# Routing weights that travel with the rows: ScalarE scales the expert results, the combining stages only add

## What is computed

```
x = LN(x + attn0(x))      # 16 heads, a band of 33 keys, a residual inside
x = LN(x + moe0(x))       # 16 experts, 4 chosen, softmax weights, GELU, hidden width 512, biases
x = LN(x + attn1(x))      # linear attention with decay, residual inside
x = LN(x + moe1(x))       # 8 experts, 2 chosen, softmax weights, SiLU gate times up, hidden width 512
# an expert layer:
#   w = softmax(top_k(logits));  result[row] = sum over k of w[row, k] * expert[topi[row, k]](x[row])
# moe1 also multiplies by 12 ** -0.5
```

## Time and profile before

| | |
|---|---|
| median of 3 runs | 1002.17 us (1000.47 to 1005.12) |
| profiled execution, its own time | 1005.16 us |
| its span, first to last instruction | 1003.3 us |
| PE busy | 737.3 us, 73% |
| DVE busy | 652.7 us, 65% |
| POOL busy | 548.0 us, 55% |
| ACT busy | 488.0 us, 49% |
| mean granted TensorE clock | 0.856 |

### The profile page before, as it was taken

One profiled execution on the slowest core, in us unless ns is written; L12 is line 12 of the kernel. 1 busy time (PEld: TensorE's weight loads), 2 busy tenths in 40 slices (PEclk: granted clock), 3 DMA queues, 4 the chain that ended last, 5 costly groups with the idle time before them and its releaser, 6 DMA issues.

```text
span 1003.3 us, 34835 instructions
## 1 busy us (share of the span) xinstructions
PE 737.3 (73%) x11638; PEld 601.2 (60%) x11639; DVE 652.7 (65%) x1988; ACT 488.0 (49%) x1174; POOL 548.0 (55%) x568
## 2 busy tenths in 40 slices
PE   2789889789987108999999991746664189999900
PEld 1466566566666107999899891634553179988900
DVE  4356667577756405777777775778775357777756
ACT  2355546456555105666666660223322257777713
POOL 1022176386568764677777772377767624445433
PEclk9799989899999558999999995776676589999965
DMA  7011121121222233343434433143332233222253
GB/s 219 2 45 35 29 73 53 39 82 50 65 68 76 69 111 81 77 87 80 89 84 87 90 66 127 51 131 100 108 104 73 86 63 67 63 53 55 51 162 99
DMA packets 135794, 78.97 MB, mean 79 GB/s; under 512 B 104338, under 2 KB 116793, under 8 KB 135696
## 3 DMA queue, kind: packets, MB, share of 16 engines
q1 hardware_dynamic: 121808, 50.97, 20.8%
q0 software_dynamic: 13312, 25.31, 8.0%
q10 hardware_dynamic: 576, 1.34, 0.4%
HBM read 32.34 MB, written 32.63 MB: 65 GB/s over the span
## 4 chain that ended last, share of the span: by engine, by line
PE 57%; DVE 13%; issue 12%; POOL 10%; ACT 3%; DMA 3%; SPq 1%; POOLq 0%; DVEq 0%; ACTq 0%
PE avbank L1676 7%; POOL xs L636 7%; PE proj L1676 7%; PE avbank L1527 4%; PE s L1655 3%; PE s L1656 3%; PE s L1657 3%; PE t L1656 3%; PE t L1655 3%; PE t L1657 3%; PE t L1721 3%; DVE nm L790 2%; PE t L1514 2%; PE proj L1433 2%; PE s L1477 2%
## 5 line engine op out<-in xcount | busy, mean ns | idle before, releaser
L702 POOL DMA_INDIRECT yt<-ysb,to_now x224 | 229.1, 1023 | 162.6 <-ACT ysb L1307 87.4
L636 POOL DMA_INDIRECT xs<-x1p,sidx x192 | 187.6, 977 | 55.2 <-issue 48.2
L930 DVE CAST h_hi<-act_out 128x512 bf16<-128x512 f32 x152 | 70.5, 464 | 77.3 <-ACT act_out L1320 74.2
L1655 PE MATMUL s<-xt,w_hi 128*128 128x256 bf16 x296 | 81.8, 276 | 42.5 <-DMA xt<-xs 42.5
L931 DVE TENSOR_TENSOR h_lo<-act_out,h_hi 128x512 bf16<-128x512 f32 x152 | 106.3, 699 | 5.2
L619 POOL TENSOR_TENSOR w_lo<-w_raw,w_hi 128x512 bf16<-128x512 f32 (+1 forms) x32 | 37.1, 1158 | 112.5 <-ACT w_hi L1291 112.2
L1221 ACT ACTIVATE prob<-t 128x384 f32<-128x384 f32 (+1 forms) x160 | 73.1, 510 | 35.8 <-PE t L1514 35.7
L1676 PE MATMUL avbank<-w_hi,h_hi 128*128 x448 | 81.1, 220 | 1.3 <-issue 0.8
L1657 PE MATMUL s<-xt,w_lo 128*128 128x256 bf16 x296 | 81.9, 277 | 0.0
L1656 PE MATMUL s<-xt,w_hi 128*128 128x256 bf16 x296 | 81.9, 277 | 0.0
L1655 PE MATMUL t<-xt,w_hi 128*128 128x256 bf16 x296 | 81.3, 275 | 0.0
(11 more groups left out here) (230 smaller groups left out, 2025.1 us busy)
## 6 DMA issues: line engine op xcount, KB each, us to landing
w_raw<-w_all SPq DMA_DIRECT2D x56, 256.0 KB
gat<-yt SPq DMA_DIRECT2D x8, 1024.0 KB, 5.8
gat<-yt SPq DMA_DIRECT2D x8, 512.0 KB, 4.2
yt<-ysb,to_now POOLq DMA_INDIRECT x224
xs<-tail_rows SPq DMA_DIRECT2D x24, 129.0 KB, 2.6
xs<-x1p,sidx POOLq DMA_INDIRECT x192, 2.8
out<-ow SPq DMA_DIRECT2D x8, 256.0 KB, 2.3
xt<-xs SPq DMA_TRANSPOSE x112
```

The lines of the kernel that those rows point to most:

```text
L636: pool.indirect_dma_start(out=xs[n][:, :], out_offset=bass.IndirectOffsetOnAxis(sidx[:, par, at:at + 1], 0), in_=x1p[:, par, t, k, :], in_ ...
L702: pool.indirect_dma_start(out=yt[n][:, :], out_offset=bass.IndirectOffsetOnAxis(to_now[:, u, s:s + 1], 0), in_=ysb[:, u, s, :], in_offset= ...
L930: ch.link(dve.tensor_copy(h_hi[:, par, c, :], act_out[:, par, c, :]))
L1655: pe.matmul(dst, w_h, xt[:, u, 0, :], start=True, stop=False)
```

## The change

Each row copy carries two 32-bit words, its number and its weight; `weigh` writes the weight into `x1p` beside the number. `load_numbers` brings both words into `to_now`. ACT's `take_out` waits for that load and scales as it takes the results out of PSUM: two instructions of 128x128 with a scale for each partition, in place of one copy of 128x256. The results in `yt` are weighted already, so that `combine` becomes three wide additions (`pair_up`: 128x1024, `add_up`: two of 128x512) and `final_sums` two additions of 128x512. `wres` and `wsel` are gone. `weigh` ends with one more `link`.

```
-XW = 2 * D + 2
+XW = 2 * D + 4
+NO = slice(2 * D, 2 * D + 2)
+WT = slice(2 * D + 2, XW)
...
-        to_now = sb("to_now", [P, RING, S2], U32)
+        to_now = sb("to_now", [P, RING, S2, 2], U32)
...
-        xs = [nc.dram_tensor(f"xs{n}", [experts[n] * REGION, XW], BF16).ap() for n in range(2)]
+        xs = [nc.dram_tensor(f"xs{n}", [experts[n] * REGION, XW // 2], U32).ap() for n in range(2)]
...
-                        sp.dma_start(to_now[:, u, :],
-                                     xs[n][bass.ds(row, TILE), 2 * D:XW].bitcast(U32).rearrange(
-                                         "(s p) o -> p (s o)", s=S2)).then_inc(to_loaded[n][u], 16)
+                        sp.dma_start(to_now[:, u, :, :],
+                                     xs[n][bass.ds(row, TILE), D:XW // 2].rearrange(
+                                         "(s p) o -> p s o", s=S2)).then_inc(to_loaded[n][u], 16)
...
+            pool.memset(tail_rows[:, :, WT], 0.0)
...
-                dve.tensor_tensor(wres[:, bass.ds(b * T, T), 0:k_n], etop[:, :, 0:k_n], bc(rsum[:, :], 2, k_n), ALU.mult)
+                ch.link(dve.tensor_tensor(x1p[:, par, :, 0:k_n, WT].bitcast(F32), etop[:, :, 0:k_n].unsqueeze(3),
+                                          bc(rsum[:, :], 2, k_n).unsqueeze(3), ALU.mult))
...
+            def add(dst, a, other):
+                return dve.scalar_tensor_tensor(out=dst, in0=a, scalar=1.0, in1=other, op0=ALU.mult, op1=ALU.add)
+
+            def pair_up(count, par):
+
+                dve.wait_ge(gathered[0][par], 16 * count)
+                ch.link(add(gat0[:, par, :, 0:2, :], gat0[:, par, :, 0:2, :], gat0[:, par, :, 2:4, :]))
+
+            def add_up(b, par):
+                ch.link(add(y[:, :, :], gat0[:, par, :, 0, :], xres[:, bass.ds(b * T, T), :]))
+                add(y[:, :, :], gat0[:, par, :, 1, :], y[:, :, :]).then_inc(comb_done, 1)
+                dve.wait_ge(comb_done, b + 1)
...
-                    combine(0, b + 2, i + 2, par, (0, 1))
+                    pair_up(i + 2, par)
...
-                    combine(0, b + 2, i + 2, par, (2, 3))
+                    add_up(b + 2, par)
...
-                for k in range(K1):
-                    for t in range(T):
-                        before = xres[:, b * T + t, :] if k == 0 else yf[:, par, t, :]
-                        ins = dve.scalar_tensor_tensor(out=yf[:, par, t, :], in0=gat1[:, b % FIN, t, k, :],
-                                                       scalar=wres[:, b * T + t, k:k + 1], in1=before,
-                                                       op0=ALU.mult, op1=ALU.add)
-                    if k < K1 - 1:
-                        ch.link(ins)
+                ch.link(add(yf[:, par, :, :], gat1[:, b % FIN, :, 0, :], xres[:, b * T:(b + 1) * T, :]))
+                ins = add(yf[:, par, :, :], gat1[:, b % FIN, :, 1, :], yf[:, par, :, :])
...
-                    nc.scalar.copy(ysb[:, u, :, :], y_bank[u % 2][:, 0:S2 * D].rearrange("p (s d) -> p s d", s=S2)
-                                   ).then_inc(y_done[n], 1)
+                    act.wait_ge(to_loaded[n][u], 16 * use + 16)
+                    for s in range(S2):
+                        ins = nc.scalar.activation(ysb[:, u, s, :], y_bank[u % 2][:, s * D:(s + 1) * D], ACT.Identity,
+                                                   scale=to_now[:, u, s, 1:2].bitcast(F32))
+                    ins.then_inc(y_done[n], 1)
```

More of the change, by code:

```diff
@@ L61 @@
 DEPTH_SCALE = 12.0 ** -0.5
-DVE_STEPS = 21
+DVE_STEPS = 22
 STACK_BANK = [1, 0] * 4
-DVE_STEPS_1 = 20
+DVE_STEPS_1 = 19
 C_IDENT, C_NEG, C_IOTA, C_BASE, C_NHALF, C_ROW, C_STEP = 0, 128, 130, 146, 162, 166, 167
@@ L265, in program @@
         gat0 = sb("gat0", [P, 2, T, K0, D])
-        wsel = sb("wsel", [P, T, K0])
         x2w = sb("x2w", [P, T, D])
@@ L494, in load_rows @@
                 def load_rows(row, u):
-                    sp.dma_start_transpose(xt[:, u, :, :], xs[n][bass.ds(row, TILE), 0:2 * D]).then_inc(xt_loaded[n][u], 16)
+                    sp.dma_start_transpose(xt[:, u, :, :], xs[n][bass.ds(row, TILE), 0:D].bitcast(BF16)).then_inc(xt_loaded[n][u], 16)
                 def load_numbers(row, u):
-                    with nc.allow_non_contiguous_dma(reason="one word of each row"):
-                        sp.dma_start(to_now[:, u, :],
-                                     xs[n][bass.ds(row, TILE), 2 * D:XW].bitcast(U32).rearrange(
-                                         "(s p) o -> p (s o)", s=S2)).then_inc(to_loaded[n][u], 16)
+                    with nc.allow_non_contiguous_dma(reason="two words of each row: its number and its weight"):
+                        sp.dma_start(to_now[:, u, :, :],
+                                     xs[n][bass.ds(row, TILE), D:XW // 2].rearrange(
+                                         "(s p) o -> p s o", s=S2)).then_inc(to_loaded[n][u], 16)
                 def numbers_of(row, u, tile, use):
@@ L570, in rows_from @@
                 for par in range(2):
-                    ins = pool.iota(x1p[:, par, :, 0:k_n, 2 * D:XW].bitcast(I32), [[P * k_n, T], [1, k_n]],
+                    ins = pool.iota(x1p[:, par, :, 0:k_n, NO].bitcast(I32), [[P * k_n, T], [1, k_n]],
                                     base=(par - 2) * L * k_n, channel_multiplier=k_n)
@@ L702, in group @@
                             pool.indirect_dma_start(
-                                out=yt[n][:, :], out_offset=bass.IndirectOffsetOnAxis(to_now[:, u, s:s + 1], 0),
+                                out=yt[n][:, :], out_offset=bass.IndirectOffsetOnAxis(to_now[:, u, s, 0:1], 0),
                                 in_=ysb[:, u, s, :], in_offset=None, bounds_check=B * L * top[n] - 1,
@@ L850, in take_ranks, with weigh @@
                                   ALU.add).then_inc(rank_used[n], 1)
-            def weigh(n, b):
+            def weigh(n, b, par):
                 e_n, k_n = experts[n], top[n]
@@ L877, in next_rows @@
             def next_rows(n, par):
-                rows = x1p[:, par, :, 0:top[n], 2 * D:XW].bitcast(I32)
+                rows = x1p[:, par, :, 0:top[n], NO].bitcast(I32)
                 dve.tensor_scalar(rows, rows, 2 * L * top[n], None, ALU.add)
@@ L947, in expert_tiles @@
                 apart(dve)
-            def combine(n, b, count, par, ks):
-                k_n = top[n]
-                if 0 in ks:
-                    ch.link(dve.tensor_copy(wsel[:, :, :], wres[:, bass.ds(b * T, T), 0:k_n]))
-                    dve.wait_ge(gathered[n][par], 16 * count)
-                for k in ks:
-                    for t in range(T):
-                        before = xres[:, b * T + t, :] if k == 0 else y[:, t, :]
-                        ins = dve.scalar_tensor_tensor(out=y[:, t, :], in0=gat0[:, par, t, k, :],
-                                                       scalar=wsel[:, t, k:k + 1], in1=before,
-                                                       op0=ALU.mult, op1=ALU.add)
-                    if k < k_n - 1:
-                        ch.link(ins)
-                    else:
-                        ins.then_inc(comb_done, 1)
-                        dve.wait_ge(comb_done, B * n + b + 1)
+            def add(dst, a, other):
[7 more added lines that the diff above has]
+                dve.wait_ge(comb_done, b + 1)
             def y_stats():
@@ L1014, in linear_body @@
                     decay_of(b + 1, 1)
-                weigh(1, b)
+                weigh(1, b, par)
                 take_ranks(1, b, rank_ps)
@@ L1083, in body @@
                         if prev == 2:
-                            weigh(0, b - 2)
+                            weigh(0, b - 2, par)
                             place(0, b - 2, par)
@@ L1116, in body @@
                     if w == 4 and not nxt:
-                        weigh(0, b - 1)
+                        weigh(0, b - 1, 1 - par)
                         take_ranks(0, b - 1, last_rk_ps)
@@ L1161, in _ @@
             mark(0)
-            weigh(0, B - 1)
+            weigh(0, B - 1, 1)
             take_ranks(0, B - 1, rk_ps)
@@ L1170, in _ @@
             dve.wait_ge(x1_kept, B)
-            combine(0, 0, 1, 0, range(K0))
+            pair_up(1, 0)
+            add_up(0, 0)
             y_stats()
             x2_apply(0)
-            combine(0, 1, 1, 1, range(K0))
+            pair_up(1, 1)
+            add_up(1, 1)
             y_stats()
```

7 lines of the change are left out of this document (3 added, 4 removed).

## The result

The changed kernel took 1011.4 us (median of 20 runs, 1002.80 to 1015.74) beside 1002.79 for the kernel before: a ratio of 1.0074 with a 95% interval of 1.0059 to 1.0089. It is slower by 0.7%, where 997.6 was forecast, and above the range of 992.0 to 1002.5. The profiled execution took 1015.74 us, the longest of the 20, so its stages are compared with those of the kernel before one by one and not by the total.

A forecast was written before the change was run, and what follows sets the result against it. PE was taken to bound layer 0, POOL's rstd the linear loop and DVE the final sums; -2.0 - 0.9 - 2.7 + 0.5 + 0.5 + 0.1 = -4.5 us from 1002.17 gave 997.6 us, range 992.0 to 1002.5 (its own 994.5 to 1000.5).

The forecast's parts named there:

- First combine: Behind layer 0, batch 0's combine falls from 4.70 to 2.69 us; 2.0 us saved, bounds 0.9 and 2.1.
- Second combine: Runs hidden under PE's scores, PE's first reads being released by ACT's `vv`; nothing saved.
- Final sums: Batch 0 saves 0.92 us, the other seven 0.38 each (2.7 us); 3.6 us saved in all.
- the loop of POOL and ACT: In the final sums, POOL waiting on ACT's `out_ready` would limit a batch to 3.44 us, not DVE's 2.90.
- The loop's combines: Linear-attention loop: six combines each about 2 us shorter, but in front of a wait for POOL; nothing gained, bounds 0 and 8.4.
- take_out: ACT's scaled pair takes 0.59 us, 0.22 more a tile, hidden except at two ends; 0.5 us lost.
- The wait for `to_now`: ACT's take-out in the experts waits for the load of numbers and weights; taken as no wait, landing at most 4.3 us.
- no table loads: Layer 0: scaling needs no other table than GELU; the rival, two loads a tile, +160 us, 1160 us, had chance 0.02.
- ACT not the bound: Layer 0: PE stays the bound; the rival, ACT at 2.91 us a tile, up to +11 us, 1009 us, had chance 0.07.
- The link in `weigh`: One more link costs 0.11 us for each of 16: 0.5 us in attention (bounds 0 and 3.2), 0.1 in the loop.
- wider rows in attention: Rows of 520 bytes for 516 in the same 192 scatters; taken to cost nothing.
- the late numbers: Rival, layer 0: take-out waits for slow loads of numbers, 0.45 us a tile, +34, so 1032 us; chance 0.05.

The follow-up runs named there:

- e17: Kernel before, with only three buffers for y and two for the statistics and scales added in the final sums: 1004.30 us, ratio 1.0017.
- e1: Changed kernel with all its additions cut into 128x128 pieces: 1004.59 us, ratio 1.0034 to the kernel before.
- e2: Changed kernel with 128x128 additions in the final sums only: 1003.97 us, ratio 1.0021 to the kernel before.
- e14: Changed kernel plus a measurement behind its end: POOL scatters beside eight 128x128 additions, with linked or unlinked DVE work ahead; run once, 1093.46 us.
- e5: Changed kernel with all additions 128x128 and the 1.0 read from SBUF instead of an immediate: 1013.47 us, ratio 1.0111 to the kernel before.
- e9: Changed kernel with the loop's sums in the order of before, a link after each four, and 128x128 final sums: 1002.3 us, ratio 0.9997.
- e15: e9 with a link after every two of the first four additions, 128x512 final sums, three buffers for y and two for scales: 997.55 us, ratio 0.9938.
- e12: Changed kernel plus a measurement behind its end: 12 forms of DVE sums beside small POOL operations or scatters; run once, 1096.69 us.

## Why the prediction was wrong, point by point

- **First combine, -2.0:** 4.70 to 2.71 us. The work was priced right, slope and all. Of its upper bound, "2.1 us", the terms that it states give 2.0 at most. The stage shows less of it: 1.1 us in this profile; 24.3 and 24.9 us with weighted sums (e17, before), 22.8 to 23.9 in all kernels with wide ones there.
- **Second combine, nothing:** not tested by itself.
- **Final sums, -3.6:** the step that failed, the loop of POOL and ACT: "That is 1.71 + 1.65 + 0.08 = 3.44 us." The mechanism was right: POOL came to be released by ACT. The 1.71 was read beside additions of 128x128 and carried over to additions of 128x512. It measured 2.58, so a batch took 4.38, 0.56 more than before where 0.38 less was forecast. With narrow additions (e1) the batch took 3.47, close to the forecast 3.44 by luck: there it was DVE's own work. From the start of the last store to the last start of `ow` the changed kernel needs 43.1 us, before 39.9 and e2 37.1: 3.2 us more where 3.6 less was forecast, half of the miss of 1011.4 - 997.6 = 13.8 us.
- **The loop's combines, nothing:** the second step that failed. "POOL's five scatters and its wait for the third weight chunk are untouched" was wrong. One of the five was held in each of six batches, for 0.2 to 0.3 us, under `add_up`. And of the three that are left from the batch before, which the prediction didn't name, the second was held for 0.74 to 0.79 us under `pair_up`, in five batches. Held time rose by 4.1 us and the loop by 2.1 us (3.4 to 4.3 in the kernels with the same loop).
- **take_out, +0.5:** the pair at 0.63 for 0.59, hidden in the steady state as forecast. At the ends too small: 0.7 us in layer 0, up to 1.4 in layer 1.
- **The wait for `to_now`, nothing; no table loads; ACT not the bound:** right. ACT was busy 161.9 us of 220 in layer 0, and the table loads are where they were.
- **The link in `weigh`, wider rows in attention:** left open. The stages behind attention add up to +6.4 us (622.2 against 615.8), the measured ratio to +7.4; a microsecond may lie in attention. To the first GELU the two kernels with before's attention took 381.8 and 382.9 us, the 17 with the change's 374.9 to 386.9, in the mean 382.2: no cost shows, but one below a microsecond or two would not.

- **The range:** the bounds of the terms, simply added, reach from some 993 to 1004 us, so "its own range" of 994.5 to 1000.5 was narrower than its working.

None of the rivals held this cause. On the slow side stood the late numbers, ACT as the bound and the table loads; the one that should have been there was that wider additions hold POOL, with `minus_mean` at 0.72 us for 0.26 and a scatter at 1.70 for 0.96 as its price.

## What to carry to other kernels

Before widening or merging DVE operations with two SBUF inputs, look at what POOL does beside them: under one addition of 0.7 to 1.2 us a 128x4 operation or a scatter ended only behind it, `minus_mean` by 0.09 us, a scatter by 0.83. If POOL is on the path, keep the additions short and put a link or a wait in between; if DVE is on the path, make them wide, and give POOL's chain a buffer more. And a duration read beside one form of work is no price beside another.

## What the runs showed of the hardware

- A held scatter ended 0.82 to 0.84 us behind the end of DVE's run, whether that was one instruction of 1.22 us, four of 128x128, eight, or (in e14) 12 to 15.
- A run of short unlinked additions can hold POOL like one long instruction: 2.18 us for eight immediate ones, 2.67 for eight with the scalar from SBUF. The rule of the Trainium skill cited above gives the lock for one instruction, which by e1's rows (an estimate) would have let POOL in after 0.2 us; the runs of e1, e5 and e14 say otherwise, and e9 and e15 that a link frees it. It is not so in every unlinked run: in e12, in the kernel before and in e14 beside the six that were held, scatters took 0.96 to 1.17 us, and what decides stays open.
- An addition of 128x128 starts 0.20 us behind the last with the immediate and 0.26 with the scalar from SBUF: (1.70 - 0.29) / 7 and (2.18 - 0.35) / 7.
- The lock works both ways: `dtop`, 0.17 us, took 2.32 under two `low_weights`.
